# A routed expert layer: outputs weighted in the tile and scattered with an adding transfer

## The reference

```python
logits = xt @ Wg.T
topk_logits, topk_idx = jax.lax.top_k(logits, TOP_K)      # 2 of 8
w = jax.nn.softmax(topk_logits, axis=-1)
gates = jnp.zeros((T, N_EXPERTS), xt.dtype).at[rows, topk_idx].add(w)
h = jax.nn.gelu(jnp.einsum('th,ehi->tei', xt, W1) + b1, approximate=False)
o = jnp.einsum('tei,eih->teh', h, W2) + b2
y = jnp.einsum('te,teh->th', gates, o)
...
x = _layernorm(x + ffn(x))
```

## Time and profile before

| | before |
|---|---|
| median of three runs | 866.33 us |
| the profiled execution | 867.0 us |
| its span | 865.2 us |
| TensorE busy | 667.6 us, 77% |
| VectorE busy | 562.7 us, 65% |
| ScalarE busy | 404.8 us, 47% |
| GpSimd busy | 339.9 us, 39% |
| DMA packets | 111.43 MB |

### The profile page before, as it was taken

How to read it: one execution, slowest core, us unless ns; L and a number is a source line. 1 busy time by engine, 2 the same in 40 slices (tenths; PEclk the granted TensorE clock), 3 DMA queues, 4 the chain that set the end, 5 groups by cost and what they waited for, 6 DMA issues and landing times. The chain is left out here.

```text
span 865.2 us, 14217 instructions
## 1 busy us (share of the span) xinstructions
PE 667.6 (77%) x5145; PEld 445.3 (51%) x5145; DVE 562.7 (65%) x942; ACT 404.8 (47%) x597; POOL 339.9 (39%) x375
## 2 busy tenths in 40 slices
PE   5596747779876887766876781689999999999910
PEld 3453512245422563223633361478888888888810
DVE  5556525567655485454833477788988888888724
ACT  4444634344452444421355132266666666666414
POOL 9122423244332443321433141525555555554225
PEclk9989968789997799766999795589999999999965
DMA  9909550069100971007110003746776666676163
GB/s 284 177 6 219 186 204 2 0 82 186 76 0 0 171 121 49 1 0 100 49 50 1 0 1 120 253 138 234 242 242 236 238 223 224 225 227 212 53 209 107
DMA packets 80235, 111.43 MB, mean 129 GB/s; under 512 B 5472, under 2 KB 67632, under 8 KB 79160
## 3 DMA queue, kind: packets, MB, share of 16 engines
q1 hardware_dynamic: 75776, 98.84, 41.1%
q0 software_dynamic: 4416, 12.06, 4.5%
HBM read 88.01 MB, written 22.87 MB: 128 GB/s over the span
## 5 line engine op out<-in xcount | busy, mean ns | idle before, releaser
L988 ACT ACTIVATE probs<-R 128x1024 f32<-128x1024 f32 (+3 forms) x128 | 86.5, 704 | 102.0 <-PE R L1229 101.8
L313 PE MATMUL HB<-xT,w 128*128 128x256 f16 x1104 | 128.4, 278 | 3.9 <-DVE xT L1803 3.9
L1578 POOL DMA_INDIRECT scratch_ys<-y,dst x46 | 83.5, 1815 | 110.3 <-DVE y L1817 103.3
L1932 PE MATMUL YB<-w,h 128*128 128x256 f16 x1104 | 124.5, 273 | 0.0
L340 DVE TENSOR_REDUCE rowmax<-G 128x1 f32<-128x384 f32 (+3 forms) x132 | 78.6, 637 | 70.1 <-PE G L330 70.1
L313 PEld LDWEIGHTS HB<-xT,w 128*128 128x128 f16 x1104 | 110.0, 100 | 18.9 <-DVE xT L1803 2.5
L1657 ACT ACTIVATE hf<-HB,b 128x256 f32<-128x256 f32 x184 | 77.3, 471 | 84.6 <-PE HB L313 84.6
L1932 PEld LDWEIGHTS YB<-w,h 128*128 128x128 f16 x1104 | 106.1, 98 | 17.2 <-issue 5.2
L929 POOL TENSOR_SCALAR_AFFINE_SELECT probs<-probs 128x256 f32<-128x256 f32 x128 | 51.6, 410 | 123.4 <-ACT probs L988 122.9
L1569 POOL DMA_INDIRECT xg<-scratch_xs,src x46 | 50.8, 1104 | 39.3 <-PE XB L1918 25.4
L1829 DVE SCALAR_TENSOR_TENSOR h<-hf,h 128x512 f16<-128x512 f32 x92 | 63.7, 693 | 3.1
(11 more groups left out here) (248 smaller groups left out, 1064.2 us busy)
## 6 DMA issues: line engine op xcount, KB each, us to landing
w1f<-in_W SPq DMA_DIRECT2D x23, 1024.0 KB, 7.4
w2f<-in_W SPq DMA_DIRECT2D x23, 1024.0 KB, 5.4
scratch_qk<-qk SPq DMA_DIRECT2D x8, 512.0 KB, 4.8
scratch_ax<-stage SPq DMA_DIRECT2D x16, 256.0 KB, 2.9
scratch_vw<-stage SPq DMA_DIRECT2D x16, 256.0 KB, 3.5
a_x<-scratch_ax SPq DMA_DIRECT2D x4, 1024.0 KB, 6.4
vw<-scratch_vw SPq DMA_DIRECT2D x4, 1024.0 KB, 4.8
parts<-scratch_ys SPq DMA_DIRECT2D x8, 512.0 KB, 7.4
```

Of the source, the lines that this page charges most:

```text
L313: last = nc.tensor.matmul(out, left(a, k), right(b, k), start=(k == 0 and m == 0), stop=(k == n - 1 and m == 2))
L988: A.activation(probs[:, n % 4, :, 0:S - 128 * j], R[slot][:, :, 0:S - 128 * j], ACT.Exp, scale=1.0 / (QS * QS)).then_inc(r.empty[slot], 1)
L1578: pool.indirect_dma_start(out=dram["ys"], in_=y[:, n % 2, t, :], in_offset=None, out_offset=bass.IndirectOffsetOnAxis(dst[:, at:at + 1], 0 ...
L1932: last = M.matmul(YB[q][:, t, :], h[:, q, a, m, t * 128:t * 128 + 128], w2[:, q, b, m, :], start=False, stop=((t, m, a) == (1, FM - 1, 1)))
```

## The change

Each output half is multiplied by its gate when VectorE writes it, and the scatter adds it in flight onto `scratch_ys`, which now has one row per token (and 128 rows for empty slots) and starts as a copy of the tokens. The last part loads that sum and normalises it; the weighing and both additions are gone.

For this the gates are worked out ahead of the wait for `ranks`, and SP stores them as two more columns of `scratch_xs`, so that the gather brings a token's values and its two gates. VectorE picks the right one with `choice` (`both`, `weight`). SP also stores the copy and a block of zeros. POOL's scatters become single halves: each waits for the landing of the one before, and the order is the first half of n - 4, gather(n), the second half of n - 4.

```diff
@@ -1417,7 +1421,7 @@
     w2 = sb("w2", [128, 2, 2, FM, D], F16)
-    xg = sb("xg", [128, 2, HALVES, D])
+    xg = sb("xg", [128, 2, HALVES, D + 2])
     xT = sb("xT2", [128, 2, 2 * DC, SLOTS], F16)
...
@@ -1495,8 +1498,15 @@
         for k in range(NT // NQ):
-            sp.dma_start(dram["xs"][k * S:(k + 1) * S, :].rearrange("(t p) d -> p t d", p=128),
+            sp.dma_start(dram["xs"][k * S:(k + 1) * S, 0:D].rearrange("(t p) d -> p t d", p=128),
                          z[:, k * NQ:(k + 1) * NQ, :]).then_inc(x_stored, 16)
+        for k in range(NT // NQ):
+            sp.dma_start(dram["ys"][k * S:(k + 1) * S, :].rearrange("(t p) d -> p t d", p=128),
+                         z[:, k * NQ:(k + 1) * NQ, :]).then_inc(sums_set, 16)
+        sp.wait_ge(zeros_set, 1)
+        sp.dma_start(dram["ys"][T:T + 128, :], zeros[:, :]).then_inc(sums_set, 16)
+        sp.wait_ge(gate_done, 1)
+        sp.dma_start(dram["xs"][:, D:].rearrange("(t p) c -> p t c", p=128), pair[:, :, :]).then_inc(x_stored, 16)
         sp.wait_ge(eid_done, 1)
...
@@ -1513,12 +1523,11 @@
-        sp.wait_ge(y_out[0], (TILES + 1) // 2 * HALVES * 16)
-        sp.wait_ge(y_out[1], TILES // 2 * HALVES * 16)
+        for t in range(HALVES):
+            sp.wait_ge(y_out[t], TILES * 16)
         for k in range(NT // NQ):
-            for c in range(2):
-                sp.dma_start(parts[:, k * NQ:(k + 1) * NQ, c, :], dram["ys"][c * T + k * S:c * T + (k + 1) * S, :]
-                             .rearrange("(t p) d -> p t d", p=128)).then_inc(parts_in[k], 16)
+            sp.dma_start(z[:, k * NQ:(k + 1) * NQ, :], dram["ys"][k * S:(k + 1) * S, :]
+                         .rearrange("(t p) d -> p t d", p=128)).then_inc(sums_in[k], 16)
         for k in range(NT // NQ):
...
@@ -1558,42 +1566,41 @@
                             ALU.mult).then_inc(halves_set, 1)
-        pool.wait_ge(x_stored, NT // NQ * 16)
+        pool.wait_ge(x_stored, (NT // NQ + 1) * 16)
...
                 pool.wait_ge(xt_full, n - 1)
+                pool.wait_ge(weight_done, n - 1)
             for t in range(HALVES):
...
-        def scatter(n):
+        def scatter(n, t):
             pool.wait_ge(y_done, n + 1)
-            for t in range(HALVES):
-                at = n * HALVES + t
-                pool.indirect_dma_start(out=dram["ys"], in_=y[:, n % 2, t, :], in_offset=None,
-                                        out_offset=bass.IndirectOffsetOnAxis(dst[:, at:at + 1], 0)
-                                        ).then_inc(y_out[n % 2], 16)
+            if n + t > 0:
+                pool.wait_ge(y_out[1 - t], (n + t) * 16)
+            at = n * HALVES + t
+            pool.indirect_dma_start(out=dram["ys"], in_=y[:, n % 2, t, :], in_offset=None,
+                                    out_offset=bass.IndirectOffsetOnAxis(dst[:, at:at + 1], 0), compute_op=ALU.add
+                                    ).then_inc(y_out[t], 16)
...
         pool.wait_ge(dst_done, 1)
+        pool.wait_ge(sums_set, (NT // NQ + 1) * 16)
         for n in range(4, TILES):
+            scatter(n - 4, 0)
             gather(n)
-            scatter(n - 4)
+            scatter(n - 4, 1)
         for n in range(TILES - 4, TILES):
-            scatter(n)
-        def add_part(k):
-            rows = slice(k * NQ, (k + 1) * NQ)
-            pool.wait_ge(part_done, k)
-            P.tensor_tensor(z[:, rows, :], z[:, rows, :], parts[:, rows, 1, :], ALU.add).then_inc(part_added, 1)
+            for t in range(HALVES):
+                scatter(n, t)
...
@@ -1670,13 +1675,6 @@
-        def weigh(k):
-            act.wait_ge(parts_in[k], 2 * 16)
-            for t in range(k * NQ, (k + 1) * NQ):
-                last = A.activation(parts[:, t, 1, :], parts[:, t, 1, :], ACT.Copy, scale=gate[:, 1, t:t + 1])
-            last.then_inc(part_done, 1)
         def normalize(k):
...
@@ -1729,6 +1726,11 @@
+        dve.wait_ge(gexp_done, 1)
+        after(V.tensor_scalar(gap[:, :], gate[:, 1, :], 1.0, None, ALU.add))
+        after(V.reciprocal(gate[:, 0, :], gap[:, :]))
+        V.tensor_copy(pair[:, :, 0], gate[:, 0, :])
+        V.tensor_tensor(pair[:, :, 1], gate[:, 1, :], gate[:, 0, :], ALU.mult).then_inc(gate_done, 1)
         dve.wait_ge(ranks, 1)
...
@@ -1782,14 +1784,12 @@
-        dve.wait_ge(gexp_done, 1)
-        after(V.tensor_scalar(gap[:, :], gate[:, 1, :], 1.0, None, ALU.add))
-        after(V.reciprocal(gate[:, 0, :], gap[:, :]))
-        after(V.tensor_tensor(gate[:, 1, :], gate[:, 1, :], gate[:, 0, :], ALU.mult))
-        after(V.scalar_tensor_tensor(dst_f[:, :], slot_map[:, 1, :], -float(T), src_f[:, :],
-                                     ALU.mult, ALU.add))
-        after(V.scalar_tensor_tensor(spare_f[:, :], slot_map[:, 1, :], 0.0, own_f[:, :], ALU.is_equal, ALU.mult))
-        V.scalar_tensor_tensor(dst_f[:, :], dst_f[:, :], 2.0 * T, spare_f[:, :], ALU.add, ALU.add).then_inc(slot_done, 1)
+        V.tensor_scalar(choice[:, :, 0], slot_map[:, 1, :], 2.0, None, ALU.is_equal)
+        V.tensor_scalar(choice[:, :, 1], slot_map[:, 1, :], 1.0, None, ALU.is_equal)
+        after(V.tensor_scalar(spare_f[:, :], slot_map[:, 1, :], 0.0, float(T), ALU.is_equal, ALU.mult))
+        after(V.scalar_tensor_tensor(dst_f[:, :], spare_f[:, :], 1.0, src_f[:, :], ALU.mult, ALU.add))
+        after(V.tensor_scalar(spare_f[:, :], slot_map[:, 1, :], 0.0, idle_f[:, 0:1], ALU.is_equal, ALU.mult))
+        V.tensor_tensor(dst_f[:, :], dst_f[:, :], spare_f[:, :], ALU.add).then_inc(slot_done, 1)
         dve.wait_ge(slot_done, 1)
...
@@ -1802,6 +1802,8 @@
                                    ALU.mult, ALU.subtract).then_inc(xt_done, 1)
+            after(V.tensor_tensor(both[:, :, :], xg[:, q, :, D:], choice[:, n * HALVES:n * HALVES + HALVES, :], ALU.mult))
+            V.tensor_reduce(weight[:, n % 4, :], both[:, :, :], AX.X, ALU.add).then_inc(weight_done, 1)
...
@@ -1812,9 +1814,14 @@
             if n >= 2:
-                dve.wait_ge(y_out[q], j * HALVES * 16)
+                for t in range(HALVES):
+                    dve.wait_ge(y_out[t], (n - 1) * 16)
+            dve.wait_ge(weight_done, n + 1)
             dve.wait_ge(y_full, n + 1)
-            V.tensor_scalar(y[:, q, :, :], YB[q][:, :, :], 1.0 / (WS * XS), None, ALU.mult).then_inc(y_done, 1)
+            for t in range(HALVES):
+                last = V.tensor_scalar(y[:, q, t, :], YB[q][:, t, :], weight[:, n % 4, t:t + 1], 1.0 / (WS * XS),
+                                       ALU.mult, ALU.mult)
+            last.then_inc(y_done, 1)
...
@@ -1847,18 +1854,9 @@
             tiles = range(k * NQ, (k + 1) * NQ)
-            if k == 0:
-                dve.wait_ge(parts_in[k], 2 * 16)
-                for t in tiles:
-                    last = V.scalar_tensor_tensor(z[:, t, :], parts[:, t, 1, :], gate[:, 1, t:t + 1], z[:, t, :],
-                                                  ALU.mult, ALU.add)
-                after(last)
-            else:
-                dve.wait_ge(part_added, k)
-            for t in tiles:
-                last = V.scalar_tensor_tensor(z[:, t, :], parts[:, t, 0, :], gate[:, 0, t:t + 1], z[:, t, :],
-                                              ALU.mult, ALU.add)
-            after(last)
+            dve.wait_ge(sums_in[k], 16)
+            if k > 0:
+                dve.wait_ge(var_done, k)
             for t in tiles:
...
@@ -2014,7 +2012,7 @@
                             ("vw", (NB * 128, 2 * PAIRS * D), F16),
-                            ("xs", (T, D), F32), ("ys", (2 * T + TILES * SLOTS, D), F32)):
+                            ("xs", (T, D + 2), F32), ("ys", (T + 128, D), F32)):
         dram[name] = nc.dram_tensor("scratch_" + name, shape, dt).ap()
```

More of the change, by code:

```diff
@@ L1394, in expert_block @@
     token_f = sb("token_f", [128, 2, NT])
-    own_i = sb("own_i", [128, TILES * HALVES], I32)
-    own_f = sb("own_f", [128, TILES * HALVES])
+    idle_f = sb("idle_f", [128, 1])
+    choice = sb("choice", [128, TILES * HALVES, 2])
+    both = sb("both", [128, HALVES, 2])
+    weight = sb("weight", [128, 4, HALVES])
+    zeros = sb("zeros", [128, D])
+    pair = sb("pair", [128, NT, 2])
     in_row = sb("in_row", [128, 2 * NT, 128], F16)
@@ L1427, in expert_block @@
     shift = sb("shift", [128, 2, NQ])
-    parts = sb("parts", [128, NT, 2, D])
     stats = sb("stats2", [128, NQ, 6])
@@ L1448, in expert_block @@
         sem("x_stored"), sem("placed"), sem("mapped"), sem("src_done"), sem("dst_done"))
+    sums_set, zeros_set, gate_done, weight_done = sem("sums_set"), sem("zeros_set"), sem("gate_done"), sem("weight_done")
     halves_found, halves_set = sem("halves_found"), sem("halves_set")
@@ L1461, in expert_block @@
     hot_done = sem("hot_done")
-    parts_in = [sem(f"parts_in{i}") for i in range(NT // NQ)]
-    part_done, part_added = sem("part_done"), sem("part_added")
+    sums_in = [sem(f"sums_in{i}") for i in range(NT // NQ)]
     var_done, pool_step, rstd_done = sem("var2_done"), sem("pool2_step"), sem("rstd2_done")
@@ L1539, in _ @@
```

(10 more changed lines are left out.)

## The result

The changed kernel is slower: **921.0 us**, median of four runs (918.8 to 926.1), against 868.5 for the kernel before beside it (865.8 to 872.0). The ratio is 1.061, with a 95% interval of 1.055 to 1.068. The forecast was 886, its range ended at 906.

What follows compares the result with a forecast made beforehand. TensorE bounds the expert tiles, period 11.34 us. From 867.0: +0.65 routing, +2.5 scatters behind the last output, -12.5 last part, +29 GpSimd's loop in the tiles = 886.6; 0.7 less for the median, 886 us. Range 854 to 906.

Steps and rivals of the forecast that it cites:

- Bound, place and mechanism: Expert tiles: second scatter held by VectorE's W2 split, then behind weight loads; gathers and transposes wait, GpSimd's loop becomes the period.
- the price of the loaded link: GpSimd's loop in a tile: a scatter landing among weight loads 6.7 us, pick-up 0.28, adding 0.5.
- I take 0.5: Each scatter: adding in flight costs 0.5 us, between bounds of 0 (plain scatter) and 2.4 (a quiet transfer again).
- My sign of a wrong whole: Scatters: the whole prediction would be wrong if an adding transfer's cost lay outside 0.35 to 2 us.
- The 0.28 of the pick-up: GpSimd between scatters: the next scatter starts about 0.28 us after the one before has landed.
- The loop of 13.1 us in 16 periods: Expert tiles: GpSimd's loop takes 13.1 us against 11.34, 1.8 us more in 16 periods, +29 us.
- My upper bound of 14.4 in 17: Expert tiles: GpSimd's loop at most 14.4 us, with a second transfer's 0.6 in the queue, in 17 periods, 53 us.
- The backlog: Behind the last output: one tile's two scatters run one after the other before the reloads, +2.5 us.
- the last part: Reloads to last normalisation: four reloads in place of eight, no additions, 16.4 us against 28.86, -12.5 us.
- VectorE's three more instructions in a tile: VectorE in a tile: choice product, reduction and output cut in two fit into its idle time, 0 us.
- the routing: Before the first expert matmul: gate arithmetic ahead of the ranks wait costs 0.35, SyncE's extra transfers 0.3, sum +0.65 us.
- gets through: Expert tiles: with adding under about 0.35 us the second scatter starts before the W2 split; 857.0 us, chance 0.37.

Runs made afterwards that it cites:

- e6: The changed kernel, but from the third tile on SyncE loads only a quarter of W1 and W2; 861.1 us.
- e2: The changed kernel with plain scatters that write and do not add, gathers still between the two scatters; 890.0 us.
- e3: The kernel before with one thing added: each scatter waits for the landing of the one before, nothing adds; 866.7 us.
- e1: The changed kernel with one scatter wait per tile, for both scatters of the tile before, and 128 own spare rows for the second half; 855.4 us, ratio 0.987.
- e5: The changed kernel with plain scatters that do not add and the gathers put ahead of both scatters; 855.7 us.
- e9: The changed kernel with plain scatters and VectorE's two long splits of W1 and W2 cut into four instructions each; 864.05 us.
- e11: The changed kernel, adding kept, with gathers ahead of both scatters and VectorE's two long splits cut into four instructions each; 903.1 us.

## Why the prediction was wrong

- **Bound, place and mechanism: right.** It named GpSimd's scatters, one landing behind the other, a scatter held in the W2 split and then behind the next weight load, and transposes waiting for `xg`. The tile at 700.06 does that, there with its first half; the second half is held up alike elsewhere (677.21, 3.13 us). That the loads are part of it is shown by e6. One reading was too strong: transfers of GpSimd don't wait until all weights are in, since from 706 to 708 us both queues moved packets.
- **The step that failed: the price of the loaded link, 6.7 + 0.28 + 0.5 = 7.5 us.** From 603.23 to 831.47 us the loop took 14.3 us in the mean, where I had 13.1. Of the two steps from scatter to scatter in a tile the shorter took 5.2 (I had 5.6), the longer, with the loaded landing, **9.1**: 8.3 to the landing and 0.77 for the pick-up. So the landing was 1.6 over the 6.7 of the plain one where I had 0.5, and the pick-up 0.77 where I had 0.28. Of the 1.6 some 0.9 is the adding, since the plain scatters of e2 in the same order took 7.4; the other 0.7 the plain ones have too.
- **"I take 0.5" for the adding** was too low in quiet as well: issue to landing went from 2.4 to 3.75, +1.35, of which +0.58 is the issue itself (1.55 in place of 0.97). The bounds of 0 and 2.4 held it, the choice between them did not. "The rest is a round trip which the read of the sum repeats in part" had no row behind it. My sign of a wrong whole, an adding outside 0.35 to 2 us, failed too: 1.35 lies inside, and the time is 15 us over the range.
- **The 0.28 of the pick-up** was read from a scatter with one wait. With the wait for the output and for the landing it is 0.73 to 0.77, in e3 0.77 and 0.27 side by side. The number of waits fits all of these; it was not varied by itself.
- **The loop of 13.1 us in 16 periods: too short and too few.** From first output to last are 298.96 us in 22 steps, the last two shorter (10.9 and 5.67): the others have a mean of (298.96 - 16.57) / 20 = 14.1. At 2.8 over 11.34 in 20 periods that is 56, as measured, where I had 1.8 in 16. My upper bound of 14.4 in 17 gave 53 and was the right size; the range cut it off, since it took in the forecast only up to 906.
- **A term was missing: TensorE's clock behind its waits.** The sum let TensorE wait and go on at full speed. 20.2 of the 56.0 us are busy time at a lower clock. The loop argument doesn't need the term (GpSimd sets the period), so it is not to be added to the above; whether the period would be shorter with the clock kept was not tried.
- **The backlog: +12.2 in place of +2.5.** I took two quiet links behind the last output. Four were left (issued from 881.34 on), at 4.5 us each: a chain longer than the period is behind by the end.
- **Right:** the last part, -12.5, in part by luck (GpSimd's root chains took 1.84 to 1.89 us where I had 2.09, and in between it stood 0.80 us waiting for VectorE, which I had not seen); VectorE's three more instructions in a tile, 0 (e1 and e5, which have them, keep 11.34 us); the routing, +0.3 for +0.65, the six transfers of SyncE at no cost. The 2.4 us after the last normalisation I had at 0.
- **The rival "gets through" was wrong in its condition.** It had an adding under 0.35 us as the decider. With no adding at all the new order still costs (e2 890.0 against e5 855.7). What had to be short was VectorE's split (e9), or one of the links had to go (e1). Its tail and its time of 857 are what e1 shows, 855.4.
- **The rule of the Trainium skill** that each DMA engine takes turns between its rows, packet by packet ("DMA: Bandwidth & Descriptors", Queues, rings and completion order), would have each scatter land in little over its quiet time. The rows after disagree again in the landing, 7.1 to 9.9 us in the loads against 3.7 in quiet, and in the packets from 704 to 706 us, of which the software queue had none; from 706 to 708 us, where both queues moved, the packets fit the rule.

Open stays what the adding does in its 1.35 us beyond the issue, and why both kinds of scatter land later still in the loads.

## What to carry to other kernels

A wait for a landing turns a transfer that nobody waited for into a link of a chain: add up, for one period, issue, landing under load and pick-up of all links, and hold the sum against the period of the bounding engine. Here two plain links made 11.3 of 11.34 us and two adding ones 12.5 in a short turn and 13.9 in the mean. When transfers must not overlap, ask which of them can touch the same rows at all: one wait per tile in place of two, and 128 more spare rows, turned +6.1% into -1.3%. And what stands behind a waiting instruction on its engine counts too, above all if it then meets another engine's long instruction.

## What the runs showed of the hardware

- An adding indirect scatter of 128 rows of 1 KB: 1.55 us to issue and 3.7 to 3.8 us to landing in quiet, against 0.97 and 2.4 for a plain one. In the short link of a tile with the gathers ahead the two are closer: 3.9 (e11) against 3.7 (e3, e5). Both kernels move the same 12.1 MB on the software queue, but in 8832 packets in place of 4416.
- An indirect issue that begins inside a two-operand VectorE split ends 0.8 to 1.5 us after it, whether it adds (700.06, 3.63 us) or not (706.40, 3.04 us). With the split cut in four, 44 of e9's 46 scatter issues took at most 1.8 us, at a cost of 0.2 us a split (2.49 for 2.29).
- From a landing to the next scatter's issue on GpSimd: 0.73 to 0.77 us behind two waits, 0.27 behind one (e3).
- TensorE's granted clock was 0.66 in the 9 us behind a wait of 3.4 us; over the expert stage 0.93 against 0.98, 20 us of busy time.
